# Attention with routed experts on one core: placement copies in another layout on two queues, pieces of work at other steps

## What is computed

```python
xn = layernorm(x)
qkv = jnp.einsum('bse,ehd->bshd', xn, w_qkv)
q, k, v = jnp.split(qkv, 3, axis=-1)
logits = where(tril, q @ k.T / sqrt(64), neg)
out = softmax(logits) @ v
attn = jnp.einsum('bshd,hde->bse', out, w_out)
h = relu(disp @ w1 + b1)
y = h @ w2 + b2
ffn = sum(gate * y[topi, pos])
return x + attn + ffn
```

## Time and profile before

| | us |
|---|---|
| median of 3 runs | 3482.34 (3477.78 to 3487.60) |
| the profiled execution, its own time | 3487.42 |
| its span | 3485.6 |
| PE busy in the span | 3096.6 |
| DVE busy | 2187.6 |
| ACT busy | 1801.7 |
| POOL busy | 1464.4 |
| mean granted TensorE clock | 0.968 |

### The profile page before, as it was taken

The page is one execution under the profiler, slowest core; times in us unless marked ns, Lnnn a source line. Parts: engine busy times, 40 slices in busy tenths (PEclk is TensorE's granted clock), DMA queues, the critical chain, the costliest instruction groups (busy, mean ns, idle before and its releaser), DMA issues.

```text
span 3485.6 us, 62630 instructions
## 1 busy us (share of the span) xinstructions
PE 3096.6 (89%) x21140; PEld 2566.4 (74%) x21141; DVE 2187.6 (63%) x5471; ACT 1801.7 (52%) x3988; POOL 1464.4 (42%) x2000
## 2 busy tenths in 40 slices
PE   5599999999779999898898999899899898898986
PEld 3489998999767777777777777777777776777764
DVE  6844443444267776667766776677767766677665
ACT  3354444454355555555555555555555555555553
POOL 2122222211145555545445554455545544455442
PEclk8799999999899999999999999999999999999998
DMA  6122222221256565656556655655655565555553
GB/s 198 32 75 73 68 73 72 74 68 42 65 123 143 133 149 129 139 122 151 121 130 146 143 126 135 157 132 124 153 137 134 116 158 130 126 122 140 128 122 84
DMA packets 344509, 408.82 MB, mean 117 GB/s; under 512 B 69712, under 2 KB 301200, under 8 KB 344208
## 3 DMA queue, kind: packets, MB, share of 16 engines
q1 hardware_dynamic: 331920, 371.37, 44.1%
q0 software_dynamic: 12288, 33.57, 3.6%
HBM read 102.80 MB, written 33.55 MB: 39 GB/s over the span
## 4 chain that ended last, share of the span: by engine, by line
PE 31%; SPq 17%; DVE 12%; DMA 8%; ACT 2%; issue 2%; POOL 0%; ACTq 0%; POOLq 0%
SPq L1069 17%; PE O L1248 12%; PE S L1213 12%; DMA pT<-squares 7%; DVE squares L1372 6%; PE T L1225 5%; DVE S L1388 4%; PE W L1170 3%; ACT pr L1292 2%; DVE res L1360 1%; DVE pT L1278 1%; DVE negm L1388 0%; DMA ql<-kk 0%; PE S L1137 0%; DMA out<-res 0%
## 5 line engine op out<-in xcount | busy, mean ns | idle before, releaser
L1458 POOL TENSOR_SCALAR pr<-pr,rinv 128x128 f32<-128x128 f32 (+7 forms) x1024 | 763.6, 747 | 1185.9 <-DVE rinv L1339 1183.5
L1292 ACT ACTIVATE pr<-S,negm 128x128 f32<-128x128 f32 (+7 forms) x1024 | 758.5, 741 | 530.9 <-DVE negm L1388 505.4
L1388 DVE CUSTOM_DVE_ANT_0 S<-S,late 128x128 f32<-128x128 f32 (+7 forms) x1024 | 776.8, 759 | 78.8 <-PE S L1213 60.0
L1248 PE MATMUL O<-pT,vv 128*64 128x256 f32 (+1 forms) x5120 | 599.0, 384 | 141.9 <-DMA pT<-squares 141.5
L1213 PE MATMUL S<-kk,qq 128*128 128x256 f32 (+2 forms) x1536 | 581.7, 381 | 128.2 <-ACT pr L1292 115.2
L1248 PEld LDWEIGHTS O<-pT,vv 128*64 128x64 f32 x5120 | 365.0, 144 | 357.3 <-DMA pT<-squares 156.7
L1213 PE MATMUL S<-kk,ql 128*128 128x256 f32 (+2 forms) x1536 | 513.1, 343 | 0.0
L1213 PEld LDWEIGHTS S<-kk,qq 128*128 128x128 f32 x1536 | 288.8, 188 | 221.5 <-issue 129.0
L1225 PE MATMUL T<-ident,pr 128*128 128x128 f32 x2688 | 420.7, 273 | 0.4 <-ACT pT L1278 0.4
L799 DVE TENSOR_TENSOR hl<-h,hh 128x512 fp32r<-128x512 f32 x256 | 191.2, 747 | 320.2 <-ACT hh L762 313.1
L1377 DVE TENSOR_TENSOR ol<-O,oh 128x256 fp32r<-128x256 f32 x256 | 108.7, 424 | 447.3 <-ACT oh L1317 444.2
(11 more groups left out here) (170 smaller groups left out, 6366.0 us busy)
## 6 DMA issues: line engine op xcount, KB each, us to landing
pT<-squares SPq DMA_DIRECT2D x1024, 128.0 KB
ql<-kk SPq DMA_DIRECT2D x256, 256.0 KB, 4.1
kk<-qq SPq DMA_DIRECT2D x128, 256.0 KB, 2.8
qq<-qq SPq DMA_DIRECT2D x128, 256.0 KB, 3.0
y<-yb SPq DMA_DIRECT2D x128, 128.0 KB, 1.7
wr<-in_L_attn_w_qkv SPq DMA_DIRECT2D x128, 128.0 KB, 2.9
x<-in_L_attn_x SPq DMA_DIRECT2D x16, 512.0 KB, 5.5
xn<-xn SPq DMA_DIRECT2D x16, 512.0 KB, 5.0
```

Of the source, the lines that this page charges most:

```text
L1248: ins = e.matmul(O[hs, a:GQ], vv[n // 2 % 2][:, kt, vs], turned_p, start=(kt == 0), stop=(kt == KT - 1))
L1292: e.activation(pr[i][:, 0:w], S[s % 2][:, off:off + w], ACT.Exp, bias=negm[:, i:i + 1], scale=-1.0, accum_out=rsum[:, i:i + 1]).then_inc(e ...
L1388: e.tensor_tensor_reduce(masked, masked, late[:, SEQ - w:], 1.0, -MASKED, ALU.add, ALU.min, negm[:, i:i + 1]).then_inc(negmax.sem, 1)
L1458: e.tensor_scalar(pr[i][:, 0:width(s)], pr[i][:, 0:width(s)], rinv[:, i:i + 1], 1.0, ALU.mult, ALU.mult).then_inc(scaled.sem, 1)
```

## The change

- The square buffer and the target (`sq`, `wide`) are laid out with the quarter outermost, so that a strip is contiguous: each DMA has 32 pieces of 4 KB in place of 128 of 1 KB. The number of bytes stays.
- SyncE issues the 12 strips of source quarters 0 to 2; POOL issues the four of quarter 3, two after its scaling of step 2 and two after that of step 3 (`place_last`). Group 3 waits for both.
- POOL's gathers go from steps 1 and 3 to 5 and 6, `weigh` from 5 to 9, `add` from 6 to 11.
- Pieces and groups run at other steps (`STEP_OF`, `BANK_OF`, `AFTER`). Group 3 is broken after six key blocks (`PART` 6): its rest runs one step later.
- DVE makes `ol` one step later, after the maximum and the reciprocal (`OL_LATER`).
- The copies are shared by a table: 11 by ACT and 5 by DVE in place of 8 and 8.

```diff
-    PART = 8
+    PART = 6
+    KEPT_BY_ACT = {0, 1, 3, 5, 7, 10, 11, 12, 13, 14, 15}
+    KEPT_BY_DVE = set(range(CHUNKS)) - KEPT_BY_ACT
-    STEP_OF = {'v0': 1, 'p0': 3, 'p1': 3, 'p2': 4, 'xn': 4, 'v1': 5, 'o2': 6, 'p3': 6, 'o3': 9, 'o0': 13, 'o1': 15}
-    BANK_OF = {'p0': 1, 'p1': 0, 'p2': 2, 'p3': 0, 'o2': 2, 'xn': 0, 'v0': 0, 'o3': 2, 'v1': 1, 'o0': 2, 'o1': 2}
+    STEP_OF = {'v0': 0, 'p0': 1, 'v1': 3, 'p1': 4, 'o2': 5, 'p2': 5, 'p3': 5, 'xn': 5, 'o3': 10, 'o0': 14, 'o1': 15}
+    BANK_OF = {'p0': 1, 'p1': 0, 'p2': 1, 'p3': 0, 'o2': 2, 'xn': 2, 'v0': 0, 'o3': 2, 'v1': 1, 'o0': 2, 'o1': 2}
-        wide = pT_odd[:].rearrange("p h k q -> p (h k q)").rearrange("p (x a r) -> p x a r", x=4, a=QUARTERS)
-        sq = sb("squares", [P, 4, QUARTERS, QT, BL])
+        wide = pT_odd[:].rearrange("p h k q -> p (h k q)").rearrange("p (a x r) -> p a x r", x=4, a=QUARTERS)
+        sq = sb("squares", [P, QUARTERS, 4, QT, BL])
-        placed = Count(sem("s_placed"), 16 * QUARTERS * QUARTERS)
+        placed = Count(sem("s_placed"), 16 * QUARTERS * (QUARTERS - 1))
+        last_placed = Count(sem("s_last_placed"), 16 * QUARTERS)
-        AFTER = [9, 14, 17, 23]
+        AFTER = [10, 12, 18, 23]
+        OH_LATER, OL_LATER = 0, 1
+        def strip(a, b):
+            to, of = slice(b * BL, (b + 1) * BL), slice(a * BL, (a + 1) * BL)
+            return wide[to, a].rearrange("p x r -> p (x r)"), sq[of, b].rearrange("p x k i -> p (x k i)")
@@ place, on SyncE
-                for a in range(QUARTERS):
+                for a in range(QUARTERS - 1):
                     for b in range(QUARTERS):
-                        e.dma_start(wide[b * BL:(b + 1) * BL, :, a, :],
-                                    sq[a * BL:(a + 1) * BL, :, b].rearrange("p x k i -> p x (k i)")).then_inc(placed.sem, 16)
+                        e.dma_start(*strip(a, b)).then_inc(placed.sem, 16)
@@ values, on PE
-                        e.wait_ge(placed.sem, placed.at(n, 16 * QUARTERS * QUARTERS))
+                        e.wait_ge(placed.sem, placed.at(n + 1, 0))
+                        e.wait_ge(last_placed.sem, last_placed.at(n + 1, 0))
@@ on DVE, ahead of keep
+                if OL_LATER:
+                    low_part(n, s)
@@ on POOL
+            def place_last(n, b):
+                if b == 0:
+                    e.wait_ge(squared.sem, squared.at(n, STEPS - WIDE))
+                    e.wait_ge(pv.sem, pv.at(n, GROUPS - 2))
+                for i in (b, b + 1):
+                    e.dma_start(*strip(QUARTERS - 1, i)).then_inc(last_placed.sem, 16)
+                if n > 0 and s in (2, 3):
+                    place_last(n - 1, 2 * (s - 2))
                 if s == 0:
                     choose(n)
-                elif s in (1, 3):
-                    fetch(n, s // 2)
-                elif s == 5:
+                elif s in (5, 6):
+                    fetch(n, s - 5)
+                elif s == 9:
                     weigh(n)
-                elif s == 6:
+                elif s == 11:
                     add(n)
```

More of the change, by code:

```diff
@@ L918, in attention_and_sum @@
         raw_q = wr[:, :, 0:HDIM]
-        wide_of = lambda h, kt, t: wide[:, 2 * h + t:2 * h + 2, :, kt * BL:(kt + 1) * BL].rearrange("p t a i -> p (t a) i")
+        wide_of = lambda h, kt, t: wide[:, :, 2 * h + t:2 * h + 2, kt * BL:(kt + 1) * BL].rearrange("p a t i -> p t a i")
         with ExitStack() as pre:
@@ L1036, in group_at @@
             return None
+        OH_LATER, OL_LATER = 0, 1
+        before = lambda n, s, d: (n, s - d) if s >= d else (n - 1, s - d + STEPS)
         ALL = [(n, s) for n in range(UNITS) for s in range(STEPS)]
         END = [(UNITS, s) for s in range(16)]
+        def strip(a, b):
+            to, of = slice(b * BL, (b + 1) * BL), slice(a * BL, (a + 1) * BL)
+            return wide[to, a].rearrange("p x r -> p (x r)"), sq[of, b].rearrange("p x k i -> p (x k i)")
         @block.sync
@@ L1264, in _, with keep @@
                     values(*group_at(n, s))
-        def keep(e, n, s, parity):
+        def keep(e, n, s, own):
             i, h = s // 2, s % 2
@@ L1270, in keep @@
                 ch = FIRST_CH[s] + x
-                if ch % 2 != parity:
+                if ch not in own:
                     continue
@@ L1277, in keep @@
                 src = T[ch % 2][:, 0:blocks * P].rearrange("p (b c) -> p b c", c=P)
-                ins = e.activation(dst, src, ACT.Copy) if parity == 0 else e.tensor_copy(dst, src)
-                ins.then_inc(kept[parity].sem, 1)
+                ins = e.activation(dst, src, ACT.Copy) if own is KEPT_BY_ACT else e.tensor_copy(dst, src)
+                ins.then_inc(kept[ch % 2].sem, 1)
         @block.scalar
@@ L1323, in _ @@
                 if 0 <= lagged(n, s)[0] < UNITS and lagged(n, s)[1] < WIDE:
-                    keep(e, *lagged(n, s), 0)
+                    keep(e, *lagged(n, s), KEPT_BY_ACT)
                 if n < UNITS:
@@ L1329, in _ @@
                         work(n, name)
-                at = group_at(n, s)
+                at = group_at(*before(n, s, OH_LATER))
                 if at and at[2] == PARTS[at[1]] - 1:
@@ L1369, in square @@
                 if x == 0 and n > 0:
-                    e.wait_ge(placed.sem, placed.at(n - 1, 16 * QUARTERS * QUARTERS))
+                    e.wait_ge(placed.sem, placed.at(n, 0))
+                    e.wait_ge(last_placed.sem, last_placed.at(n, 0))
                 e.wait_ge(scaled.sem, scaled.at(n, s + 1))
-                e.transpose(sq[:, x % 2 * 2 + x // 2, :, 0:KT, :],
+                e.transpose(sq[:, :, x % 2 * 2 + x // 2, 0:KT, :],
                             pr[slot(n, s)][:, 0:KT * P].rearrange("p (k b i) -> p b k i", b=QUARTERS, i=BL)).then_inc(squared.sem, 1)
@@ L1377, in group, with low_part @@
                 e.tensor_tensor(ol[g % 2][:], O[:], oh[g % 2][:].bitcast(F32), ALU.subtract).then_inc(olo.sem, 1)
+            def low_part(n, s):
+                at = group_at(*before(n, s, OL_LATER))
+                if at and at[2] == PARTS[at[1]] - 1:
+                    group(at[0], at[1])
             for name in BEFORE:
@@ L1393, in _ @@
                     reciprocal(UNITS - 1, STEPS - 1)
+                if OL_LATER:
+                    low_part(n, s)
                 if 0 <= lagged(n, s)[0] < UNITS and lagged(n, s)[1] < WIDE:
-                    keep(e, *lagged(n, s), 1)
+                    keep(e, *lagged(n, s), KEPT_BY_DVE)
                 if 0 <= squaring(n, s)[0] < UNITS and squaring(n, s)[1] >= WIDE:
@@ L1400, in _ @@
                         work(n, name)
-                at = group_at(n, s)
-                if at and at[2] == PARTS[at[1]] - 1:
-                    group(at[0], at[1])
+                if OL_LATER == 0:
+                    low_part(n, s)
         @block.gpsimd
@@ L1473, in _ @@
                     total(n)
+            place_last(UNITS - 1, 0)
+            place_last(UNITS - 1, 2)
 def program(nc, x, w_qkv, w_out, wg, w1, b1, w2, b2, out):
```

## The result

The changed kernel took 3332.6 us (median of 4 runs, 3328.75 to 3335.69), the kernel before 3484.97 in the same session: a ratio of 0.956 (95% interval 0.9533 to 0.9587), 152 us less. The forecast was 3319 us, 163 less.

The account below looks back on a forecast made before the run. Placement and squares were taken to set the pace, PE alone needing 34.5 us a unit. Squares 5.8, placement 12.2, PE 17.7, spread 0.5 and clock 0.2 gave 36.4 us, times 63 units: 3319 us; own range 3265 to 3385, overall 3205 to 3440.

Parts of the forecast that it names:

- The placement as the term that decides: Loop stretch from SyncE's first strip issue to group 3: 13.4 us falls to 12.2, ends 10.9 and 13.8.
- the three clocks: Inside the placement, beside each other: SyncE's strips land by 10.0 to 10.9 us, POOL's by 10.3 to 11.2; DMA engines slowest.
- The rival that POOL's issue is dear: POOL's direct issues in the placement at 2.2 us each: placement 15.7 us, unit 40.4, 3572 us; chance 0.09.
- So larger pieces give nothing by these rows: Strip transfer on the DMA engines: 4 KB pieces at 4.6 us a MB, 9.6 us, against 4.4 and 9.3 before.
- The squares, 5.8: DVE from the end of step 15's scores to its last square: 6.1 us falls to 5.8, one copy going to ACT.
- PE's gap of 1.16 us: PE's idle ahead of step 1's scores: v0's products, 1.5 us, cover it; no term of the loop.
- 18.3 becomes 17.7: PE from group 3 to the end of step 15's scores: the 0.62 us gap at step 10 goes.
- Beside ACT's 21.53 busy it is hidden: ACT's three extra copies are hidden in a 37.80 us unit; without that cover some 1 us a unit.
- The clock: PE's clock over the stage: of 0.7 us a unit lost to lower clock, 0.2 is left.
- PE as the bound (3207): Rival: all strips land within 11.0 us and a unit takes 34.6 us, set by PE's work; chance 0.15.
- the transfer stays at 13.4: Rival: the placement's transfer is the bound and keeps its length, unit 38.1 us, 3427 us; chance 0.17.
- The sum: One unit of the loop: 5.8 + 12.2 + 17.7 = 35.7 us, with 0.5 spread and 0.2 clock 36.4.

Follow-up runs that it names:

- a quarter of the bytes: Changed kernel with each strip moving a quarter of its bytes, the rest of the target cleared once, issues and waits the same: 3231.78 us, ratio 0.9303.
- the last experiment: Changed kernel with the copies shared as before, even chunks by ACT and odd ones by DVE: 3464.23 us, ratio 0.9922.

## Why the prediction was right, and where it was off

**The placement as the term that decides: right.** 12.2 us forecast with 0.5 for the spread, so 12.7 on average; 12.13 measured. With it alone nearly the whole gain is there (0.9569), without it nearly nothing (0.9934). That the engines are the slowest of the three clocks held too (a quarter of the bytes: 0.9303), and that the gathers' transfer, 10% of the engines in the earlier trace rows, had to leave the stretch (92 us).

**The clocks ahead of it were both off, and it did not matter.** POOL's direct issue costs 0.52 us, not 1.2: the nearest row, the gather, was twice too dear, and even the lower bound of 0.65 lay above it. The rival that POOL's issue is dear fell with it. The port lock of the Trainium skill's page (SBUF — State Buffer, "SBUF: two separate sides") showed in no issue beside a busy DVE (at most 0.59 us), nor in the landings (2.4 to 5.7 us, SyncE's 2.3 to 6.0); no row tells whether DVE ran here in a mode that takes the port. SyncE's twelve take 9.1 us, not 7.8: in 51 of 64 units one issue, in 50 of them the sixth or a later one, takes over 1.5 us (at most 2.26). Full engines alone do not explain it: the kernel before has such an issue in 4 units of 64, the quarter of the bytes in 11. Why is open.

**"So larger pieces give nothing by these rows": wrong**, 20 us in the kernel before, 29 in the changed one. The row was kk <- qq, 4.6 us a MB, in a window of one lone copy with its ramps; the packed transfer needed 4.2 in the changed kernel's unit against 4.4 in that of before. Over 63 units (1.2 to 11.0 us behind the first issue) it is 4.2 against 4.4 with 1 KB in the changed kernel, but 4.2 with either size in the kernel before, where the engines were instead busy 0.94 of the time with 4 KB and 0.91 with 1 KB. So a lower cost of a MB is only a part of the gain.

**The squares, 5.8: right** (5.7; with the copy back, in the last experiment, 6.1). **PE's gap of 1.16 us: right**, it left and paid nothing in the loop, as said.

**"18.3 becomes 17.7" is the step that failed.** The idle ahead of `ol` went, the waits for exponentials fell to 2.7 us, and PE does end the scores of step 15 17.85 us behind the start of group 3. But the stretch is 18.4, because DVE takes them 0.55 us later. The prediction had "the scores of step 15 end where DVE takes them", which was so before (0.04 us) and no longer is: from step 13 on DVE works with no gap, and moving group 1's product ahead of step 13 took the work from PE under which DVE was hidden. I took a gain at step 10 through to the maximum of step 15 without asking which engine leads between them; DVE's 11.19 of 11.80 us before would have shown it. That the placement as a whole with the old tables has 18.3 us there, and DVE takes the scores 0.04 us after their end, fits this; group 1 alone back at its step was not tried. `ol` would stand ahead of that stretch but for its shift by a step; undoing the shift gives 32 us, of which only some 0.16 us a unit, 10 us, are outside the placement.

**"Beside ACT's 21.53 busy it is hidden": half of it.** ACT did hide its three copies. But I weighed only what ACT gets and not what DVE loses; in the changed order that is worth up to 132 us. Since the order came as a whole, the forecast did not suffer.

**The clock: nearly right.** I had 0.2 of the 0.7 us a unit remain. The time at 1.2 GHz fell from 92 to 38 us; half of it over 63 units, the same estimate as above, is 0.3 in place of 0.7.

**The rivals.** PE as the bound (3207) is what a quarter of the bytes gives (3231.78), not the real transfer. That the transfer stays at 13.4, with the Trainium skill's rule that issuing from several engines saves the issue time alone (DMA: Bandwidth & Descriptors, "Issuing engines are not separate DMA queues"), did not hold for the edit as a whole: the whole placement is 128 us faster than the layout alone. Of that some 90 are the gathers', though, so for the second queue by itself some 40 us remain (a difference of experiments, not one of its own). That is small, and so far the rule agrees. But when the strips start on POOL matters as much (53 us for one step earlier), and there the engines had more bytes moved in the same stretch, which the rule does not cover.

**The sum: right, partly because two terms cancel.** The mean unit is 36.51 for 36.4. Its placement is 0.57 under the forecast's 12.7; all the rest is 24.38 (36.51 - 12.13) for 23.7 (5.8 + 17.7 + 0.2 of clock), 0.68 over. The first is mostly the transfer of the 2.10 MB at 4.2 in place of 4.6 us a MB (0.8 us), the second the 0.7 of the failed step. Had only one of them come, the forecast would have been some 40 us off in either direction.

## What to carry to other kernels

Write the loop down engine by engine and mark on each stretch who works without a gap: only there does a saved microsecond count, and a gap closed elsewhere reappears as the next wait. A stretch that ends when one engine takes the other's result has two ends: compare when the result is ready with when it is taken (0.04 us here before, 0.55 after). Long waits of PE cost more than their length, since stretches at half the clock follow them: 113 us at 1.2 GHz with the gathers back, 38 in the change, 14 with POOL a step earlier. When a transfer sets the pace, first ask what else uses the DMA engines in that stretch, on any queue and also just behind it; here moving two gathers away (some 90 us), starting the second queue one step earlier (some 50) and holding back the copies behind it (some 130 with eight strips on each queue) were worth more than the shape of the pieces (20 to 29 us).

## What the runs showed of the hardware that I had not expected

- A direct DMA of 128 KB costs POOL 0.49 to 0.59 us in 32 pieces and 0.55 to 0.65 in 128, half of its gather of 128 rows (1.04 to 1.09 us), beside a busy DVE too.
- Transfers on two queues share the 16 engines in such a way that copies that follow on one queue delay strips on the other: the placement takes 13.07 us, and 11.81 for the same sixteen strips with the copies held back.
- SyncE's issue of a strip takes 0.51 us at least and 2.26 at most in the changed kernel. Of its 51 issues over 1.5 us 31 are the twelfth of their placement.
